# Second attention: keys in banks of 424, 424 and 254, and the context's sums over the whole third bank

## The chip, the core and the metric

The kernel runs on one NeuronCore of a Trainium2 chip, as one program. The metric is device microseconds (us) of one execution. The engines of the core are named as in the profile: PE is TensorE's matmul side, PEld its weight loads, DVE VectorE, ACT ScalarE, POOL GpSimd, SP SyncE. PSUM is the memory that PE writes, 128 partitions of eight banks; a bank holds 512 float32 columns, and one matmul writes inside one bank.

## What is computed

The program is a transformer of two layers over `x` (2 batches x 1024 tokens x 256): attention to a context of 77 tokens, a mixture of experts, a second attention, and a second mixture. The change touches the second attention alone. Cut to what matters, the reference is:

```python
xn = layernorm(ctx);  ln = layernorm(latents)            # 77 context tokens, 1024 latents
q  = (ln @ Wq)                                           # 16 heads of 64
kv = concatenate([xn @ Wkv, ln @ Wkv], axis=1)           # keys and values: 77 + 1024
qn = rmsnorm(q, qn_g) * scale;  kn = rmsnorm(k, kn_g)
sim  = einsum('bhid,bhjd->bhij', qn, kn)
sim  = where(padded_mask, sim, max_neg)                  # the mask covers the 77 context keys only
attn = softmax(sim, axis=-1)
out  = einsum('bhij,bhjd->bhid', attn, v) @ Wout + bout
```

In the kernel the order of the keys is the other way round: first the 1024 latents, then the 77 of the context, 1101 in all (`KEYS`), padded by one zero column to 1102 (`W2`).

## The kernel before

**Tiling.** `layer1_attention` works on a pair of heads at a time: 2 batches x 8 pairs of heads are 16 "pairs". A pair has 16 units (`UNITS`); a unit is 128 queries of one head against all 1101 keys. The pairs are written out for the first and the last of a batch and run in a hardware loop for those between (`all_pairs`), so 4 of the 16 pairs are written-out code and 12 are loop code. In each pair the body goes over `u` = 0, 2, ... 14. I call one such pass a step and name it by its `u`: "step 8" is the pass with u = 8. The scores that it makes are those of units u+2 and u+3, so eight steps of two units make a pair, and 128 steps the attention.

**A unit's way.** Scores lie in a `slot` of three banks, and there are two slots, one for even and one for odd units.
1. PE, `score` (L1689): three column ranges, 0 to 512, 512 to 1024 and 1024 to 1102, one for each bank. Each takes two matmuls in float32r with the same stationary operand (the high and the low part of the keys as moving operand), so a unit has four matmuls of 512 columns and two of 78. After each range `bank_filled` goes up by one.
2. DVE, `peak` (L1880, L1882): the largest score of a row. One reduction over bank 0 (512 columns) as soon as one range is there, one over the other 589 as soon as three are, and a third small one over the two results, negated, into `npeak`.
3. ACT, `exponentials` (L1823, L1824): exp(score - peak) of 1024 latents with their sum (`latent_sum`), then of the 77 context keys without one.
4. DVE, `row_sum` (L1912): masked sum over the 77, added to `latent_sum`.
5. PE, `turn` (L1696, L1698): nine transposes of the probabilities back into the same slot; DVE `copy_first` (L1903) copies tiles 0 to 3 and ACT `copy_rest` (L1835) tiles 4 to 8 into `probT`.
6. PE, `weigh` (L1714): the values weighed by `probT`, a group of four units late, half a group in each step.

**Order of a step on PE** (written out by hand): turn(u), an output projection (L1731), turn(u+1), score(u+2), score(u+3), a piece of the next pair's projections (`FRONT`), weigh, another piece (`BEHIND`). score(u+2) waits until both copies of unit u have left the slot, score(u+3) until both of unit u+1 have (`probT_act`, `probT_dve`).
**On ACT:** copy_rest(u), copy_rest(u+1), the exponentials of u+2, the FRONT piece, the exponentials of u+3, the BEHIND piece.
**On DVE:** row_sum(u), row_sum(u+1), copies (in steps 2, 6, 10 and 14 `copy_sums`, L1927, stands ahead of them, and ACT's copy_rest(u) waits for it by `r_out`), peak(u+2), peak(u+3), in some steps `invert`, and the FRONT piece.

**The pieces share one bank**, `side`: PE fills it, ACT or ACT and DVE empty it, and the next piece on PE waits for that. Four of the steps have a BEHIND piece whose bank is emptied only in the same step, behind the exponentials of unit u+2:

- step 6: FRONT `Kta`, BEHIND `V0`. `V0` (L1639) waits for DVE's L1890, which waits for ACT's L1818.
- step 8: FRONT `Ktb`, BEHIND `V1`, the same way.
- step 10: FRONT `Ktc` (77 keys), BEHIND `Qta` (L1675), the same way.
- step 12: FRONT `Qtb`, BEHIND `V2`. `V2` waits for ACT's L1803. Behind L1803 POOL makes L1601 and L1603.

Steps 0 and 2 have FRONT and BEHIND pieces too, but of the longer kind; steps 4 and 14 have a FRONT piece only. The last pair has no pieces.

```python
FRONT = {0: "Ka", 2: "c", 4: "Qb", 6: "Kta", 8: "Ktb", 10: "Ktc", 12: "Qtb", 14: "V3"}
BEHIND = {0: "Kb", 2: "Qa", 6: "V0", 8: "V1", 10: "Qta", 12: "V2"}
```

Of the kernel before, what the change touches and what calls it, by code (L numbers as in the profile page):

```python
# [17 lines left out]
ALU = mybir.AluOpType  # L18
# [37 lines left out]
KT_TILES = SEQ // P + 1  # L56
PAIRS = H1 // 2
# [120 lines left out]
class Context:  # L178


    def __init__(self, nc, ctx):
        sb = lambda n, s, d=F32: ctx.enter_context(nc.sbuf_tensor(f"a1_{n}", s, d))
        self.ctxT = sb("ctxT", [P, EC, BATCH * CTX])
        self.valid = sb("valid", [CTX, BATCH])
        self.gamma = sb("gamma", [P, 1])
        self.maskf = sb("maskf", [P, BATCH, CTX])
        self.maskn = sb("maskn", [P, BATCH, CTX])
        self.lng, self.lnb = sb("lng", [P, EC]), sb("lnb", [P, EC])


class ContextPrelude:
# [35 lines left out]
    def statistics(self, dve):  # L227
        s, v, C = Steps(dve, self.step), self.nc.vector, self.C
        dve.wait_ge(self.loaded, 144)
        s.mark(v.tensor_copy(C.maskf[:, :, :], self.mask[:, :, :]))  # L230
# [1218 lines left out]
def layer1_attention(nc, I, xres, ident, C, latT, W, w_loaded, gates, y_rows):  # L1449
# [7 lines left out]
    with phase(nc) as outer:  # L1457
# [6 lines left out]
        ctxT, valid, gamma, maskf = C.ctxT, C.valid, C.gamma, C.maskf  # L1464
# [18 lines left out]
        part_peak = sb("part_peak", [P, 2, 2])  # L1483
        latent_sum = sb("latent_sum", [P, 2])
        masked = sb("masked", [P, CTX])
# [9 lines left out]
        sums, py = slot[0][:, SEQ + P:SEQ + 3 * P], slot[1][:, SEQ + P:SEQ + P + E]  # L1495
# [10 lines left out]
        NSET = 3  # L1506
        FOLDS = D1.bit_length() - 1
# [125 lines left out]
        def _(pe):  # L1633
# [44 lines left out]
            def score(pair, u):  # L1678
# [8 lines left out]
                for lo, hi in ((0, BANK), (BANK, SEQ), (SEQ, W2)):  # L1687
                    for part in range(2):
                        ins = t_.matmul(out[:, lo:hi], q, KHL[:, pair.parity, h, part, lo:hi],  # L1689
                                        start=part == 0, stop=part == 1)  # L1690
                    ins.then_inc(bank_filled, 1)
# [93 lines left out]
        def _(act):  # L1785
# [34 lines left out]
            def exponentials(pair, u):  # L1820
                act.wait_ge(peaked, pair.g * UNITS + (u + 1))
                bias = npeak[:, u % 2:u % 2 + 1]
                a_.activation(prob[:, u % 2, 0:SEQ], slot[u % 2][:, 0:SEQ], ACT.Exp, bias=bias, accum_out=latent_sum[:, u % 2:u % 2 + 1])  # L1823
                a_.activation(prob[:, u % 2, SEQ:KEYS], slot[u % 2][:, SEQ:KEYS], ACT.Exp, bias=bias).then_inc(exped, 1)  # L1824
# [40 lines left out]
        def _(dve):  # L1865
# [8 lines left out]
            def peak(pair, u):  # L1874
# [3 lines left out]
                for i, (lo, hi, banks) in enumerate(((0, BANK, 1), (BANK, KEYS, 3))):  # L1878
                    dve.wait_ge(bank_filled, n + banks)
                    v.tensor_reduce(part[:, i:i + 1], slot[u % 2][:, lo:hi], AX.X, ALU.max).then_inc(part_peaked, 1)  # L1880
# [25 lines left out]
            def row_sum(pair, u):  # L1906
# [5 lines left out]
                v.tensor_tensor_reduce(masked[:, :], prob[:, u % 2, SEQ:KEYS], maskf[:, pair.b, :], 1.0,  # L1912
# [193 lines left out]
```

## Time and profile before

| | |
|---|---|
| median of 3 runs | 2143.6 us (2143.26 to 2143.99) |
| the profiled execution | 2148.2 us, of which 2146.4 us are its span |
| PE / PEld busy, of the span | 1923.6 us (90%) / 1652.1 us (77%) |
| DVE / ACT / POOL busy, of the span | 1272.3 us (59%) / 1022.2 us (48%) / 609.7 us (28%) |
| granted clock of TensorE, mean | 0.941 |

The second attention is the long middle part of the span, where its lines run from about 630 to 1750 us. Busy times of matmuls overlap, since they are pipelined: the start of one weight load to the start of the next tells what a matmul costs in a row of them, its own duration does not. A timeline row gives start and length of a run of like instructions, their count, and in brackets the idle time of the engine before them and what ended it. What waits for what inside a step can be read as distances from the start of the step's first score load; I call that moment S.

### The profile page before, as it was taken

The numbers are of one execution on the slowest core, as the hardware profiler recorded it, in microseconds if no ns is written. First come the engines' busy times: TensorE is split into PE (matmuls) and PEld (weight loads), VectorE is DVE, ScalarE is ACT, GpSimd is POOL, SyncE is SP. The second block draws the span as 40 slices with busy tenths as digits, with TensorE's granted clock in tenths as the row PEclk, the third lists the DMA queues.
The fourth block names the chain that finished last, engine by engine and source line by source line (L and its number), as shares of the span: only waits on it lengthen the run. The fifth ranks groups of instructions, "written<-read, shape, count | busy, mean of one in ns | idle before, by whom it ended". The sixth has DMA issues, their size and how long they took to land. (4 is left out here: it accounts for less than half of the span.)

```text
span 2146.4 us, 40118 instructions
## 1 busy us (share of the span) xinstructions
PE 1923.6 (90%) x13656; PEld 1652.1 (77%) x13657; DVE 1272.3 (59%) x2963; ACT 1022.2 (48%) x1747; POOL 609.7 (28%) x555
## 2 busy tenths in 40 slices
PE   4788957999569999999999999999999984899994
PEld 2477956999558887888888888878888863899994
DVE  5174054676656776777776677767777775122223
ACT  2543413555236555555555555555555641444441
POOL 2300002333244323432343224322433201222220
PEclk9899957999769999999999999999999995999997
DMA  5502163111242123211321132213211208211113
GB/s 201 176 28 82 64 239 104 47 49 46 84 106 53 38 51 71 54 42 47 70 54 43 45 70 63 47 33 70 64 45 33 63 23 298 90 37 34 39 35 130
DMA packets 93663, 159.24 MB, mean 74 GB/s; under 512 B 22385, under 2 KB 54831, under 8 KB 91707
## 3 DMA queue, kind: packets, MB, share of 16 engines
q1 hardware_dynamic: 82875, 134.32, 22.2%
q0 software_dynamic: 8320, 20.65, 3.2%
q8 instruction: 101, 1.65, 0.3%
q10 hardware_dynamic: 2304, 2.10, 0.3%
q14 instruction: 63, 0.52, 0.1%
HBM read 71.57 MB, written 32.41 MB: 48 GB/s over the span
## 5 line engine op out<-in xcount | busy, mean ns | idle before, releaser
L1880 DVE TENSOR_REDUCE a_part_peak<-a_slot 128x1 f32<-128x512 f32 (+1 forms) x512 | 352.6, 728 | 41.2 <-PE a_slot L1689 40.8
L1823 ACT ACTIVATE a_prob<-a_slot,a_npeak 128x1024 f32<-128x1024 f32 x256 | 286.0, 1117 | 176.5 <-DVE a_npeak L1882 176.2
L1689 PE MATMUL a_slot<-a_KHL,a_QHL 128*128 128x512 f32 (+1 forms) x1536 | 319.9, 358 | 2.3 <-ACT a_latT L1257 2.3
L1689 PEld LDWEIGHTS a_slot<-a_KHL,a_QHL 128*128 128x128 f32 x1536 | 261.9, 191 | 48.7 <-ACT a_latT L1257 2.6
L1714 PE MATMUL a_po<-a_probT,a_V 128*64 128x256 f32 (+1 forms) x2304 | 276.8, 385 | 0.0
L1835 ACT ACTIVATE a_probT<-a_slot 128x640 f32<-128x640 f32 x256 | 180.7, 706 | 200.2 <-PE a_slot L1698 182.1
L1698 PE MATMUL a_slot<-ident,a_prob 128*128 128x128 f32 x2048 | 266.1, 273 | 0.0
L1698 PEld LDWEIGHTS a_slot<-ident,a_prob 128*128 128x128 f32 x2048 | 233.7, 142 | 8.5 <-issue 0.2
L1639 PE MATMUL a_side<-a_W,a_latT 128*128 128x128 f32 x1536 | 214.1, 291 | 13.5 <-DVE a_KT L1890 5.8
L1639 PEld LDWEIGHTS a_side<-a_W,a_latT 128*128 128x128 f32 x1536 | 190.0, 199 | 45.9 <-DVE a_KT L1890 19.2
L1714 PEld LDWEIGHTS a_po<-a_probT,a_V 128*64 128x64 f32 (+1 forms) x2304 | 154.0, 136 | 82.2 <-issue 10.3
L1903 DVE COPY a_probT<-a_slot 128x512 f32<-128x512 f32 x256 | 176.7, 690 | 29.8 <-PE a_slot L1698 28.7
L1912 DVE CUSTOM_DVE_ANT_0 a_masked<-a_prob,a_maskf,a_latent_sum 128x77 f32<-128x77 f32 x256 | 124.6, 487 | 117.4 <-ACT a_prob L1824 100.2
L1068 PEld LDWEIGHTS m1e_ph<-m1e_xT,m1e_w 128*128 128x128 f32 x1248 | 148.7, 196 | 8.6 <-DMA m_down<-in_L_ffn_W_dram 3.6
L1068 PE MATMUL m1e_ph<-m1e_xT,m1e_w 128*128 128x128 f32 x1248 | 149.2, 279 | 6.1 <-DMA m_down<-in_L_ffn_W_dram 3.4
L1068 PEld LDWEIGHTS m0e_ph<-m0e_xT,m0e_w 128*128 128x128 f32 x1248 | 147.9, 195 | 6.0 <-ACT m0e_w L1095 3.3
L1068 PE MATMUL m0e_ph<-m0e_xT,m0e_w 128*128 128x128 f32 x1248 | 148.4, 278 | 3.4 <-ACT m0e_w L1095 2.9
L1077 PE MATMUL m1e_py<-m_down,m1e_h 128*128 x624 | 141.0, 379 | 0.0
L1580 POOL TENSOR_TENSOR a_square<-a_knat 128x1152 f32<-128x1152 f32 x15 | 31.6, 2108 | 368.0 <-ACT a_V L1808 368.0
L1133 DVE TENSOR_TENSOR m1e_h<-m1e_ph,m_bup 128x1024 f32<-128x1024 f32 x39 | 47.8, 1225 | 142.8 <-PE m1e_ph L1068 142.8
L1077 PEld LDWEIGHTS m1e_py<-m_down,m1e_h 128*128 128x128 f32 x624 | 115.6, 190 | 14.1
L1586 POOL TENSOR_TENSOR a_square<-a_square 128x576 f32<-128x576 f32 (+3 forms) x180 | 104.2, 579 | 14.1
(319 smaller groups left out, 2884.8 us busy)
## 6 DMA issues: line engine op xcount, KB each, us to landing
a_KHL<-a_KT SPq DMA_DIRECT2D x128, 256.0 KB, 4.5
a_QHL<-a_QT SPq DMA_DIRECT2D x128, 128.0 KB, 2.3
m_up<-_L_ffn_gate_up_proj_dram SPq DMA_DIRECT2D x8, 1024.0 KB, 8.7
m_up<-in_L_ffn_W_dram SPq DMA_DIRECT2D x8, 1024.0 KB, 9.1
m_down<-in_L_ffn_W_dram SPq DMA_DIRECT2D x8, 1024.0 KB, 12.5
a_prob_dram<-a0p_zeros SPq DMA_DIRECT2D x4, 1632.0 KB
a_dist_dram<-a_dist SPq DMA_DIRECT2D x4, 1632.0 KB, 8.1
a_band_prob<-a_prob_dram SPq DMA_DIRECT2D x4, 1632.0 KB, 6.8
```

Source lines behind the costliest of these rows:

```text
L1068: ins = nc.tensor.matmul(ph[:, q, cols], w[:, q, c, cols], xT[:, c, :], start=c == 0, stop=c == EC - 1)
L1077: ins = nc.tensor.matmul(py[1 - q][:, 0:E], a[:, 1 - q, f * P:(f + 1) * P], down[:, bass.ds(e, 1), f, :].rearrange("p a n -> p (a n)"), st ...
L1586: g_.tensor_tensor(half[:, :, 0:w], half[:, :, 0:w], half[:, :, w:2 * w], ALU.add).then_inc(summed, 1)
L1639: ins = t_.matmul(out, x[:, c, :], W[:, parity, i, c, :], start=c == 0, stop=c == EC - 1)
L1689: ins = t_.matmul(out[:, lo:hi], q, KHL[:, pair.parity, h, part, lo:hi], start=part == 0, stop=part == 1)
L1698: ins = t_.transpose(out[:, j * P:(j + 1) * P], prob[:, u % 2, j * P:(j + 1) * P], ident[:, :])
L1714: ins = t_.matmul(po_t[h * D1:(h + 1) * D1, :], V[0:rows, pair.parity, j, h, :], probT[0:rows, gi % 2, j, h, :], start=j == PARTS[0][0], s ...
L1823: a_.activation(prob[:, u % 2, 0:SEQ], slot[u % 2][:, 0:SEQ], ACT.Exp, bias=bias, accum_out=latent_sum[:, u % 2:u % 2 + 1])
L1835: a_.activation(probT[:, u // 4 % 2, HALF:KT_TILES, h, u % 2 * P:(u % 2 + 1) * P], slot[u % 2][:, HALF * P:KT_TILES * P].rearrange("p (t q ...
L1880: v.tensor_reduce(part[:, i:i + 1], slot[u % 2][:, lo:hi], AX.X, ALU.max).then_inc(part_peaked, 1)
L1903: v.tensor_copy(probT[:, u // 4 % 2, 0:HALF, h, u % 2 * P:(u % 2 + 1) * P], slot[u % 2][:, 0:HALF * P].rearrange("p (t q) -> p t q", q=P)) ...
L1912: v.tensor_tensor_reduce(masked[:, :], prob[:, u % 2, SEQ:KEYS], maskf[:, pair.b, :], 1.0, latent_sum[:, u % 2:u % 2 + 1], ALU.mult, ALU.a ...
```

## The change

The columns of a unit's scores are cut at 424 and 848 in place of 512 and 1024 (`CUT` = 424), so that the three banks hold 424, 424 and 254 columns; 253 of the last (`REST`) are keys, 176 latents and the 77 of the context. The place of a bank in the slot stays. With that:

- `score` has four matmuls of 424 columns and two of 254 a unit; their number stays.
- `peak` reduces banks 0 and 1 in one instruction (2 x 424 into two results) once **two** ranges are there, where it was 512 once one was there; then the 253 of the third bank once three are there; then the three results.
- The first exponential takes 848 columns from two banks, with their sum, the second 253.
- `row_sum` works on 253 probabilities in place of 77. Its mask, `maskr`, has ones for the 176 latents, set once by a memset long before.
- `sums` and `py`, which borrow the end of a slot's third bank, move to its last 256 columns, clear of the 254.

Nothing stands in another order on any engine. The diff, cut to its core:

```diff
+CUT = 424
+REST = KEYS - 2 * CUT
...
-        s.mark(v.tensor_copy(C.maskf[:, :, :], self.mask[:, :, :]))
+        s.mark(v.memset(C.maskr[:, :, 0:REST - CTX], 1.0))
+        s.mark(v.tensor_copy(C.maskf, self.mask[:, :, :]))
...
-        sums, py = slot[0][:, SEQ + P:SEQ + 3 * P], slot[1][:, SEQ + P:SEQ + P + E]
+        sums, py = slot[0][:, 3 * BANK - 2 * P:], slot[1][:, 3 * BANK - E:]
...
+        def two_banks(x):
+            return x[:, 0:2 * BANK].rearrange("p (n k) -> p n k", n=2)[:, :, 0:CUT]
...
-                for lo, hi in ((0, BANK), (BANK, SEQ), (SEQ, W2)):
+                for i, (lo, hi) in enumerate(((0, CUT), (CUT, 2 * CUT), (2 * CUT, W2))):
                     for part in range(2):
-                        ins = t_.matmul(out[:, lo:hi], q, KHL[:, pair.parity, h, part, lo:hi],
+                        ins = t_.matmul(out[:, i * BANK:i * BANK + hi - lo], q, KHL[:, pair.parity, h, part, lo:hi],
                                         start=part == 0, stop=part == 1)
                     ins.then_inc(bank_filled, 1)
...
-                a_.activation(prob[:, u % 2, 0:SEQ], slot[u % 2][:, 0:SEQ], ACT.Exp, bias=bias, accum_out=latent_sum[:, u % 2:u % 2 + 1])
-                a_.activation(prob[:, u % 2, SEQ:KEYS], slot[u % 2][:, SEQ:KEYS], ACT.Exp, bias=bias).then_inc(exped, 1)
+                a_.activation(prob[:, u % 2, 0:2 * CUT].rearrange("p (n k) -> p n k", n=2), two_banks(slot[u % 2]),
+                              ACT.Exp, bias=bias, accum_out=latent_sum[:, u % 2:u % 2 + 1])
+                a_.activation(prob[:, u % 2, 2 * CUT:], slot[u % 2][:, 2 * BANK:2 * BANK + REST], ACT.Exp, bias=bias).then_inc(exped, 1)
...
-                for i, (lo, hi, banks) in enumerate(((0, BANK, 1), (BANK, KEYS, 3))):
-                    dve.wait_ge(bank_filled, n + banks)
-                    v.tensor_reduce(part[:, i:i + 1], slot[u % 2][:, lo:hi], AX.X, ALU.max).then_inc(part_peaked, 1)
+                dve.wait_ge(bank_filled, n + 2)
+                v.tensor_reduce(part[:, 0:2], two_banks(slot[u % 2]), AX.X, ALU.max).then_inc(part_peaked, 1)
+                dve.wait_ge(bank_filled, n + 3)
+                v.tensor_reduce(part[:, 2:3], slot[u % 2][:, 2 * BANK:2 * BANK + REST], AX.X, ALU.max).then_inc(part_peaked, 1)
...
-                v.tensor_tensor_reduce(masked[:, :], prob[:, u % 2, SEQ:KEYS], maskf[:, pair.b, :], 1.0,
+                v.tensor_tensor_reduce(masked[:, :], prob[:, u % 2, 2 * CUT:], maskr[:, pair.b, :], 1.0,
                                        latent_sum[:, u % 2:u % 2 + 1], ALU.mult, ALU.add,
```

## Rows read from the trace of the kernel before

**Rows 1.** Windows, the attention's steady stretch: bounds and length, busy, granted clock, DMA

```profile
700.00:1746.00 1046.00, 1035.24 (x7781) 857.42 (x7780) 769.81 (x1858) 588.42 (x1164) 360.72 (x308) 1.00 0.22 51
```

**Rows 2.** Waits, same stretch: engine and line, for whom, us in all, times, longest

```profile
PEld a_side L1639 <- DVE a_KT L1890: 14.5, 28, 0.7
```

**Rows 3.** Groups by form, same stretch: count, busy us, mean ns, idle before

```profile
L1880 DVE TENSOR_REDUCE a_part_peak<-a_slot 128x1 f32<-128x512 f32 x239 | 165.1, 691 | 25.9 <-PE a_slot L1689 25.6
L1880 DVE TENSOR_REDUCE a_part_peak<-a_slot 128x1 f32<-128x589 f32 x239 | 183.1, 766 | 0.0
L1823 ACT ACTIVATE a_prob<-a_slot,a_npeak 128x1024 f32<-128x1024 f32 x238 | 265.9, 1117 | 162.9 <-DVE a_npeak L1882 162.7
L1824 ACT ACTIVATE a_prob<-a_slot,a_npeak 128x77 f32<-128x77 f32 x238 | 77.5, 326 | 0.0
```

**Rows 4.** Line L1689 (ns min/median/max), then its third, sixth and seventh load in step 8

```profile
L1689 PE MATMUL a_slot<-a_KHL,a_QHL x1536: 197/392/775, 633.2 to 1746.1; 128*128 128x512 f32 x128, 128*128 128x78 f32 x64
...
1102.80 0.19 PEld L1689 LDWEIGHTS a_slot<-a_KHL,a_QHL 128*128 128x128 f32 x1
...
1103.51 0.19 PEld L1689 LDWEIGHTS a_slot<-a_KHL,a_QHL 128*128 128x128 f32 x1
...
1103.62 0.19 PEld L1689 LDWEIGHTS a_slot<-a_KHL,a_QHL 128*128 128x128 f32 x1
```

**Rows 5.** Timeline, step 8 of a loop pair, from its first score load: start, us

```profile
1102.46 2.39 PEld L1689 LDWEIGHTS a_slot<-a_KHL,a_QHL 128*128 128x128 f32 x12
...
1102.77 0.71 ACT L1835 ACTIVATE a_probT<-a_slot 128x640 f32<-128x640 f32 x1 [0.71 <-PE a_slot L1698]
...
1103.23 1.40 DVE L1880 TENSOR_REDUCE a_part_peak<-a_slot 128x1 f32<-128x512 f32 x2 [0.20 <-PE a_slot L1689]
...
1104.85 1.12 ACT L1823 ACTIVATE a_prob<-a_slot,a_npeak 128x1024 f32<-128x1024 f32 x1 [1.38 <-DVE a_npeak L1882]
```

**Rows 6.** Timeline, step 8, its end: the keys' low part and V1

```profile
1106.79 0.69 DVE L1890 TENSOR_TENSOR a_KT<-a_side,a_KT 128x512 fp32r<-128x512 f32 x1 [0.32 <-ACT a_KT L1818]
...
1107.54 0.63 PEld L1639 LDWEIGHTS a_side<-a_W,a_latT 128*128 128x128 f32 x5 [0.66 <-DVE a_KT L1890]
```

**Rows 7.** Timeline, step 6: S, the keys' low part and V0

```profile
1093.94 2.39 PEld L1689 LDWEIGHTS a_slot<-a_KHL,a_QHL 128*128 128x128 f32 x12
...
1098.27 0.69 DVE L1890 TENSOR_TENSOR a_KT<-a_side,a_KT 128x512 fp32r<-128x512 f32 x1
...
1099.17 0.63 PEld L1639 LDWEIGHTS a_side<-a_W,a_latT 128*128 128x128 f32 x5 [0.38 <-DVE a_KT L1890]
```

**Rows 8.** Timeline, step 10: S, the context keys' low part and Qta

```profile
1111.04 2.39 PEld L1689 LDWEIGHTS a_slot<-a_KHL,a_QHL 128*128 128x128 f32 x12
...
1115.28 0.23 DVE L1890 TENSOR_TENSOR a_KT<-a_side,a_KT 128x77 fp32r<-128x77 f32 x1
...
1115.90 0.42 PEld L1675 LDWEIGHTS a_side<-ident,a_qnat 128*128 128x128 f32 x4 [0.39 <-issue]
```

**Rows 9.** Timeline, step 12 to the S of step 14

```profile
1118.69 2.39 PEld L1689 LDWEIGHTS a_slot<-a_KHL,a_QHL 128*128 128x128 f32 x12
...
1122.40 0.69 ACT L1803 ACTIVATE a_qgam<-a_side,a_gamma 128x512 f32<-128x512 f32 x1
...
1123.49 0.97 PEld L1639 LDWEIGHTS a_side<-a_W,a_latT 128*128 128x128 f32 x8 [0.39 <-ACT a_qgam L1803]
...
1124.28 1.27 POOL L1603 TENSOR_TENSOR a_QT<-a_qgam,a_QT 128x512 fp32r<-128x512 f32 x1
...
1124.43 1.22 DVE L1912 CUSTOM_DVE_ANT_0 a_masked<-a_prob,a_maskf,a_latent_sum 128x77 f32<-128x77 f32 x1 [1.58 <-ACT a_prob L1824]
...
1126.11 0.71 ACT L1835 ACTIVATE a_probT<-a_slot 128x640 f32<-128x640 f32 x1 [1.03 <-DVE a_rT L1927]
...
1127.03 2.36 PEld L1689 LDWEIGHTS a_slot<-a_KHL,a_QHL 128*128 128x128 f32 x12
```

**Rows 10.** Timeline, step 14 to the next turn

```profile
1132.72 0.14 PEld L1696 LDWEIGHTS a_slot<-ident,a_prob 128*77 128x77 f32 x1 [0.38 <-ACT a_prob L1824]
```

More of the change, by code:

```diff
@@ L185, in __init__ @@
         self.gamma = sb("gamma", [P, 1])
-        self.maskf = sb("maskf", [P, BATCH, CTX])
+        self.maskr = sb("maskr", [P, BATCH, REST])
+        self.maskf = self.maskr[:, :, REST - CTX:]
         self.maskn = sb("maskn", [P, BATCH, CTX])
@@ L1463, in layer1_attention @@
         sem = lambda n: nc.alloc_semaphore(f"a1_{n}")
-        ctxT, valid, gamma, maskf = C.ctxT, C.valid, C.gamma, C.maskf
+        ctxT, valid, gamma, maskr = C.ctxT, C.valid, C.gamma, C.maskr
         W2 = KEYS + 1
@@ L1482, in layer1_attention @@
         probT = sb("probT", [P, 2, KT_TILES, 2, 2 * P])
-        part_peak = sb("part_peak", [P, 2, 2])
+        part_peak = sb("part_peak", [P, 2, 3])
         latent_sum = sb("latent_sum", [P, 2])
-        masked = sb("masked", [P, CTX])
+        masked = sb("masked", [P, REST])
         rsum = sb("rsum", [P, 2, 2, 2])
```

## Prediction

> **What bounds the kernel now.** I read the windows first: in the attention's steady stretch PE is busy 1035 of 1046 us, at the full clock (1.00, the 2.4 GHz level), DVE 770 and ACT 588 [rows 1]. So a step is as long as PE's work in it, unless PE waits inside. The waits tell where it does: 28 times for DVE's L1890, 14.5 us in all [rows 2]. That is the bank `side`, in steps 6 and 8 of 14 pairs. The timeline then shows how near the others are. I measure from S, the start of a step's first score load, and take a loop pair, as 12 of the 16 are.
>
> **What PE saves.** In step 8 the third load starts at 1102.80, the sixth at 1103.51, so a 512-column matmul costs 0.71/3 = 0.235 us; the sixth to the seventh load, behind 78 columns, 0.11; the unit takes 1103.62 - 1102.46 = 1.16 [rows 4, 5]. The 0.11 is the pace of the loads, since 78 columns themselves need less: the durations are 392 ns (512) and 197 ns (78) at the same latency, so a column costs 195/434 = 0.449 ns, and 78 columns some 0.04 [rows 4]. A matmul of 424 then costs 0.235 - 88 x 0.449 ns = 0.195, one of 254 0.04 + 176 x 0.449 ns = 0.116. The change takes 4 x 0.040 = 0.16 from a unit and adds 2 x 0.005, leaving 1.01. Its idea is in this: columns are moved from matmuls that cost by the column to ones that cost the load's pace. Two units a step save 0.30, 128 steps 38 us, if nothing else binds.
>
> **What takes some of it at once: score(u+3).** It waits for ACT's copy of unit u+1, which starts 0.31 behind S and ends at 1102.77 + 0.71 = S + 1.02 [rows 5]. From an end to PE's next load I take 0.06, as from L1890's end, 1107.48, to V1's load, 1107.54 [rows 6]. So the second unit can't start before S + 1.08; now it starts at S + 1.16, afterwards it would like S + 1.01. Both units end at 1.08 + 1.01 = 2.09, where it was 2.33 or 2.34: a step saves 0.25, not 0.30. In the four written-out pairs the copy starts some 0.06 later, and the saving is 0.19.
>
> **What the Vector chain adds.** DVE's first reduction starts at S + 0.77, when bank 0 is filled [rows 5]. Afterwards it waits for four matmuls in place of two. Before, the second matmul streamed until third load + 0.235 = S + 0.34 + 0.235 = 0.575. Afterwards the fourth streams from 0.11 + 3 x 0.195 = 0.695 until 0.89. The start moves by 0.31, to S + 1.08. The work behind it stays: 691 + 766 ns for 589 + 512 columns [rows 3] become, at the slope of these two (75 ns for 77 columns), 1.02 + 0.44, the same 1.46. The exponentials too: 1117 + 326 ns give 0.835 ns a column, so 0.97 + 0.47, the same sum [rows 3]. So all that stands behind the first peak (the exponentials from S + 2.39 [rows 5], L1818, L1890, L1803) comes 0.31 later, counted from S, while PE comes 0.25 earlier. Where the two meet inside a step, the step ends by the late one:
>
> - **Step 6.** L1890 ends at 1098.96, V0 is loaded at 1099.17, S + 5.23: a slack of 0.21, 0.15 with the 0.06 [rows 7]. Afterwards V0 can be loaded at 5.02 + 0.31 + 0.06 = 5.39. The step gets 0.16 **longer**.
> - **Step 8.** PE waits already; all of the 0.31 is added: 0.31 **longer** [rows 6].
> - **Step 10.** L1890 ends at 1115.51 = S + 4.47, Qta at S + 4.86 [rows 8]. Afterwards 4.84: 0.02 shorter.
> - **Step 12.** L1803 ends at 1123.09 = S + 4.40, V2 at S + 4.80 [rows 9]. Afterwards V2 can go at 4.77: 0.03 shorter. But there is a longer chain: L1803, then POOL's L1601 and L1603, the latter until 1125.55; DVE's row_sum, two inputs in SBUF, takes 1.22 us and ends at 1125.65, 0.10 behind POOL [rows 9]. I read that as DVE waiting for POOL's end. Then L1927 and ACT's copy_rest(u), which ends at 1126.82, 0.21 ahead of the next S (1127.03) [rows 9]. Afterwards POOL ends 0.31 later, and row_sum has 176 more columns, at 0.97 ns 0.17 more: 0.48 in all against a slack of 0.21 - 0.06. The step gets 0.33 **longer**. With S this late, ACT's copy of the second unit no longer binds in step 14, which saves 0.31.
> - **Steps 0, 2, 4, 14.** The turn or piece at the end waits for nothing near: in step 14 the turn comes at 1132.72 = S + 5.69 [rows 10], its exponentials end near S + 3.8, 4.1 afterwards, and the second unit's about 1.6 later, when turn(u+1) is a further 1.3 off. They save 0.25 each, 14 saves 0.31.
>
> The last chain hangs on what row_sum waits for. If its 1.22 us were not POOL's doing, POOL's shift would not reach PE, step 12 would get 0.03 shorter like step 10, and the sum below would be 15 x 0.36 = 5.4 us lower.
>
> The page SBUF — State Buffer of the Trainium skill (SBUF: two separate sides) states that a DVE instruction with two SBUF inputs and a GpSimd one that reads SBUF share one port as an exclusive lock, held for the whole instruction, whoever comes first. By that rule the longer row_sum can also hold POOL up, which speaks against the change; the end 0.10 behind POOL's agrees with it.
>
> **The sum.** A loop pair: -3 x 0.25 - 0.31 + 0.16 + 0.31 - 0.02 + 0.33 = -0.28. Twelve: -3.4. The three written-out pairs with pieces: the saving of steps 0, 2, 4 is 0.19 and of 14 0.25, so -0.04 each, -0.1. The last pair has no pieces: 7 x -0.19 = -1.3, and -0.3 for the two first units. The memset is outside and short. Together -5 us: the 38 are there, and 33 of them go again. Against the profiled execution of 2148.2 us that is 2143.2; against the median, which I forecast, 2143.6 - 5.0 = **2138.6**.
>
> What no row shows is bounded. A reduction and an exponential that read two banks with a gap: nothing more than by the column, or, as the 589 columns that cross a bank already cost no more than the slope, at most a tenth of a us each. I take nothing; each tenth on the chain costs four steps of fifteen pairs, 60 x 0.1 = +6 us. The row_sum of 253: from 0 (hidden behind POOL) to twice the slope, so step 12 gets 0.16 to 0.50 longer: -2.5 to +2.5 us. POOL's chain could also not bind at all: -5. A 254-column matmul: 0.11 to 0.13, 0 to +2 us.
>
> **Rivals.**
> - *PE's gain arrives.* If ACT and DVE were not in the way (the reduction starts early enough, the bank `side` is emptied in time), each step saves 0.25 to 0.30: -32 to -38 us, 2106 to 2112. For it: PE's 99% [rows 1]. Against it: V1 starts 0.06 behind L1890 already now [rows 6].
> - *The Vector chain takes more than PE gives: slower.* The place is the first reduction and exponential in steps 6 to 12; the price is 60 times what each extra amount e adds to the 0.31. At e = 0.08 the gain is gone, from e = 0.15 it is slower by over 0.2%; e = 0.2 gives 2138.6 + 12 = 2151. For it: two-bank patterns, a third partial result, a longer DVE instruction against POOL. Against it: the columns are the same and so is the number of instructions.
> - *Narrow float32r matmuls cost more a column.* If 254 columns took 0.22, what a 512-column one takes, the unit would be back at 1.22, the four free steps longer by 0.12, and steps 6 to 12 as long as reckoned or more: some +1.4 a pair, near 2165. Against it: the 78-column duration, which leaves room for one pass only [rows 4].
> - *The change does nothing*: the widths are in the code as it says; no chance worth a number.
>
> **How the numbers follow.** The forecast has 0.70, with its own range 2129 to 2147 by the bounds above; 0.37 of it lies under 2139.3, 0.31 within 0.2%, 0.02 above. The gain arriving in full or half: 0.10. The slower chain: 0.17, of which 0.12 over 2147.9 and 0.05 under. The narrow matmuls: 0.03. A measurement of this kernel can tell about 0.2%, 4.3 us, from no change. Faster 0.47, same 0.36, slower 0.17. The range of 2123 to 2152 leaves out the full gain, the narrow matmuls and the ends of the rest.
>
> **What the profile after would show.** Score loads 0.195 apart and 0.115 behind 254 columns, or not (rival 3). The second unit's first load at S + 1.08, behind ACT's copy. The first reduction at S + 1.08 and about 1.02 long; more would be e. PE waiting for L1890 in steps 6 and 8 with 28 waits that total some 14.5 + 28 x 0.4 = 26 us or more, and for L1803 and r_out's copy in step 12. Steps 6, 8 and 12 longer than before and 0, 2, 4, 14 shorter. It is wrong if steps 6 and 8 get shorter, or if the first exponential starts elsewhere than S + 2.70.

## The result, and the profile after

| | before | after |
|---|---|---|
| median | 2144.7 us (2143.3 to 2147.1, 6 runs) | 2154.2 us (2151.1 to 2156.8, 6 runs) |
| the profiled execution | 2148.2 us, span 2146.4 | 2153.8 us, span 2152.0 |
| first to last unit of the attention | 1110.7 us | 1115.2 us |

The change makes the kernel slower: the ratio is 1.0037, interval 1.0025 to 1.0048. Forecast were 5 us less; it became 8 us more by the ratio, 9.4 by the two medians, and 2154.2 lies above the range. ("First to last unit" is from the first load of the first unit's scores to that of the last two units.)

The windows row of the stretch of [rows 1], in the trace of after (bounds and length; busy us of PE, PEld, DVE, ACT, POOL; granted clock; DMA share and GB/s):

```profile
700.00:1746.00 1046.00, 1013.90 (x7754) 864.40 (x7754) 803.63 (x1850) 583.59 (x1158) 367.20 (x309) 1.00 0.23 51
```

PE is busy 21 us less than before, at the same clock, in a stretch of the same length. So the gain of the narrower matmuls is there, and PE stands idle for it: 32 us in place of 11. Where, the waits say (engine and line, for whom; us in all, times, longest; same stretch):

```profile
PEld a_side L1649 <- DVE a_KT L1902: 28.4, 28, 1.2
ACT a_probT L1846 <- DVE a_rT L1939: 23.4, 15, 1.6
```

The first answers to [rows 2]: the same 28 waits for the keys' low part, 28.4 us for 14.5. The second is `copy_rest(u)` waiting for the copy of 1/sum, which stands behind the row sum on DVE: 1.6 us at most, and 1.0 before.

The groups by form that answer to [rows 3] (count | busy us, mean ns | idle before):

```profile
L1890 DVE TENSOR_REDUCE a_part_peak<-a_slot 128x2 f32<-128x848 f32 x238 | 247.8, 1041 | 61.7 <-PE a_slot L1699 61.7
L1892 DVE TENSOR_REDUCE a_part_peak<-a_slot 128x1 f32<-128x253 f32 x237 | 97.1, 410 | 0.0
L1833 ACT ACTIVATE a_prob<-a_slot,a_npeak 128x848 f32<-128x848 f32 x237 | 229.8, 969 | 201.5 <-DVE a_npeak L1894 201.3
L1835 ACT ACTIVATE a_prob<-a_slot,a_npeak 128x253 f32<-128x253 f32 x236 | 111.2, 471 | 0.0
L1924 DVE CUSTOM_DVE_ANT_0 a_masked<-a_prob,a_maskr,a_latent_sum 128x253 f32<-128x253 f32 x237 | 161.6, 682 | 84.2 <-ACT a_prob L1835 69.7 <-issue 14.1
L1934 DVE COPY a_rwide<-a_rsum 128x256 f32<-128x256 f32 x59 | 21.1, 358 | 2.0
```

The reductions (1.04 and 0.41 us) and the exponentials (0.97 and 0.47) have the durations forecast; a gap between two banks costs nothing. The last two rows are the ones to keep in mind: the mean of the row sum contains some that take three times the usual, and the copy into `rwide`, which the change doesn't touch, has a mean of 358 ns.

**Step by step.** In what follows a step's length is the distance from its S to the next S, the median of the twelve loop pairs, in us. Worked out from the score loads of each trace:

| step | 0 | 2 | 4 | 6 | 8 | 10 | 12 | 14 | pair |
|---|---|---|---|---|---|---|---|---|---|
| before | 10.59 | 9.84 | 8.75 | 8.51 | 8.58 | 7.64 | 8.35 | 8.08 | 70.32 |
| forecast change | -0.25 | -0.25 | -0.25 | +0.16 | +0.31 | -0.02 | +0.33 | -0.31 | -0.28 |
| after, change | -0.26 | -0.20 | -0.26 | **+0.34** | +0.29 | +0.04 | **+0.46** | -0.29 | +0.13 |

Six of the eight are within 0.06 of the forecast. Steps 6 and 12 make 0.31 of the 0.41 us that the pair is above it.

Step 6 in the trace of after (timeline, a loop pair; answers to [rows 7]):

```profile
1095.66 2.14 PEld L1699 LDWEIGHTS a_slot<-a_KHL,a_QHL 128*128 128x128 f32 x12
...
1099.16 3.95 POOL L1596 TENSOR_TENSOR a_square<-a_square 128x512 f32<-128x512 f32 x6
...
1099.99 0.59 DVE L1934 COPY a_rwide<-a_rsum 128x256 f32<-128x256 f32 x1
...
1100.50 0.68 DVE L1902 TENSOR_TENSOR a_KT<-a_side,a_KT 128x512 fp32r<-128x512 f32 x1
...
1101.23 0.97 PEld L1649 LDWEIGHTS a_side<-a_W,a_latT 128*128 128x128 f32 x8 [0.93 <-DVE a_KT L1902]
```

The copy into `rwide` takes 0.59 us, and the keys' low part stands behind it on DVE. And the same stretch before, where the copy takes 0.29:

```profile
1096.66 3.85 POOL L1586 TENSOR_TENSOR a_square<-a_square 128x512 f32<-128x512 f32 x6
...
1097.98 0.29 DVE L1922 COPY a_rwide<-a_rsum 128x256 f32<-128x256 f32 x1
```

Of POOL's six folds the first runs in both kernels for 1.27 us: before from 1096.66 to 1097.93, so that the copy fell 0.05 behind its end; after from 1099.16 to 1100.43, across the copy's start.

Step 12 of the same pair in the trace of after (timeline; answers to [rows 9]):

```profile
1121.08 2.14 PEld L1699 LDWEIGHTS a_slot<-a_KHL,a_QHL 128*128 128x128 f32 x12
...
1125.07 0.69 ACT L1813 ACTIVATE a_qgam<-a_side,a_gamma 128x512 f32<-128x512 f32 x1
...
1126.95 1.28 POOL L1613 TENSOR_TENSOR a_QT<-a_qgam,a_QT 128x512 fp32r<-128x512 f32 x1
...
1127.10 1.41 DVE L1924 CUSTOM_DVE_ANT_0 a_masked<-a_prob,a_maskr,a_latent_sum 128x253 f32<-128x253 f32 x1 [1.40 <-ACT a_prob L1835]
...
1128.43 0.41 DVE L1939 COPY a_rT<-a_slot 128x256 f32<-128x256 f32 x1
...
1128.96 0.70 ACT L1846 ACTIVATE a_probT<-a_slot 128x640 f32<-128x640 f32 x1 [1.58 <-DVE a_rT L1939]
...
1129.89 1.19 PEld L1699 LDWEIGHTS a_slot<-a_KHL,a_QHL 128*128 128x128 f32 x7 [0.55 <-issue]
```

The chain is the one that the prediction describes, L1813, POOL's QT, the row sum, the copy of 1/sum, copy_rest, and now PE is idle 0.55 us ahead of the scores.

### The profile page after: what moved, and what is told of

It is laid out like the page before. It is cut to its first block and busy times, and to the rows that moved or that the text cites. A ratio compares the mean times of both kernels' runs of the same rounds, so it can differ in the third digit from the quotient of the medians.

```text
span 2152.0 us, 40077 instructions
## 1 busy us (share of the span) xinstructions
PE 1905.9 (89%) x13656; PEld 1664.5 (77%) x13657; DVE 1312.9 (61%) x2964; ACT 1018.9 (47%) x1747; POOL 616.1 (29%) x555
## 5 line engine op out<-in xcount | busy, mean ns | idle before, releaser
L1833 ACT ACTIVATE a_prob<-a_slot,a_npeak 128x848 f32<-128x848 f32 x256 | 248.2, 969 | 217.7 <-DVE a_npeak L1894 217.4
L1890 DVE TENSOR_REDUCE a_part_peak<-a_slot 128x2 f32<-128x848 f32 x256 | 266.4, 1041 | 79.7 <-PE a_slot L1699 79.6
L1699 PE MATMUL a_slot<-a_KHL,a_QHL 128*128 128x424 f32 (+1 forms) x1536 | 298.9, 343 | 6.3 <-ACT a_probT L1846 3.7
L1699 PEld LDWEIGHTS a_slot<-a_KHL,a_QHL 128*128 128x128 f32 x1536 | 268.6, 190 | 17.5 <-issue 6.7
L1924 DVE CUSTOM_DVE_ANT_0 a_masked<-a_prob,a_maskr,a_latent_sum 128x253 f32<-128x253 f32 x256 | 171.8, 671 | 90.6 <-ACT a_prob L1835 76.1
L1835 ACT ACTIVATE a_prob<-a_slot,a_npeak 128x253 f32<-128x253 f32 x256 | 120.6, 471 | 0.0
```

The lines of the kernel that those rows point to most:

```text
L1699: ins = t_.matmul(out[:, i * BANK:i * BANK + hi - lo], q, KHL[:, pair.parity, h, part, lo:hi], start=part == 0, stop=part == 1)
L1833: a_.activation(prob[:, u % 2, 0:2 * CUT].rearrange("p (n k) -> p n k", n=2), two_banks(slot[u % 2]), ACT.Exp, bias=bias, accum_out=latent ...
L1835: a_.activation(prob[:, u % 2, 2 * CUT:], slot[u % 2][:, 2 * BANK:2 * BANK + REST], ACT.Exp, bias=bias).then_inc(exped, 1)
L1890: v.tensor_reduce(part[:, 0:2], two_banks(slot[u % 2]), AX.X, ALU.max).then_inc(part_peaked, 1)
L1924: v.tensor_tensor_reduce(masked[:, :], prob[:, u % 2, 2 * CUT:], maskr[:, pair.b, :], 1.0, latent_sum[:, u % 2:u % 2 + 1], ALU.mult, ALU.a ...
```

## The experiments

Theory (formed once the profile after was read): the whole chain behind the first peak comes 0.3 us later, as forecast, and two places where DVE and POOL wait for each other add what was not reckoned. Rival: something general, so that reductions, exponentials or row sums are slower in all steps. Each table row below gives the change against before, by step, as above.

| | 0 | 2 | 4 | 6 | 8 | 10 | 12 | 14 | pair | first to last unit | median, ratio |
|---|---|---|---|---|---|---|---|---|---|---|---|
| after | -.26 | -.20 | -.26 | +.34 | +.29 | +.04 | +.46 | -.29 | +.13 | 1115.2 | 2154.2, 1.0037 [1.0025, 1.0048] |
| after_again | -.25 | -.20 | -.24 | +.34 | +.29 | +.04 | +.46 | -.28 | +.16 | 1115.0 | 2151.2, 1.0035 [1.0021, 1.0048] |
| late_first | .00 | .00 | .00 | +.29 | +.44 | +.20 | +.44 | .00 | +1.37 | 1134.3 | 2172.3, 1.0124 [1.0105, 1.0144] |
| three_reductions | -.25 | -.20 | -.25 | +.07 | -.03 | -.20 | +.15 | -.29 | -1.00 | 1094.2 | 2134.0, 0.9939 [0.9921, 0.9958] |
| sum_77 | -.26 | -.20 | -.24 | +.15 | +.29 | +.04 | +.28 | -.28 | -.22 | 1105.8 | 2145.9, 0.9998 [0.9985, 1.0011] |
| invert_behind | -.26 | -.20 | -.24 | +.14 | +.29 | -.20 | +.46 | -.29 | -.31 | 1109.5 | 2145.6, 0.9995 [0.9981, 1.0010] |
| three_invert | -.26 | -.20 | -.26 | -.18 | -.03 | -.20 | +.14 | -.29 | -1.28 | 1093.4 | 2130.7, 0.9935 [0.9916, 0.9955] |
| pool_short | -.26 | -.20 | -.24 | +.33 | +.30 | +.04 | -.12 | -.25 | -.38 | 1109.3 | 2144.1, 0.9996 [0.9978, 1.0015] |
| row_late | -.25 | -.20 | -.24 | +.33 | +.29 | +.62 | -.12 | -.24 | +.20 | 1114.5 | 2152.3, 1.0030 [1.0017, 1.0044] |
| row_late_14 | -.26 | -.20 | -.26 | +.34 | +.29 | +.04 | -.12 | -.25 | -.40 | 1107.4 | 2145.5, 0.9998 [0.9985, 1.0012] |
| before_moves | .00 | .00 | .00 | .00 | .00 | .00 | -.04 | +.01 | -.03 | 1113.6 | 2147.4, 1.0008 [0.9994, 1.0021] |
| best_14 | -.25 | -.20 | -.24 | -.18 | -.03 | -.20 | -.24 | -.25 | -1.59 | 1089.9 | 2124.1, 0.9899 [0.9881, 0.9918] |

The time outside the attention varies from profile to profile between 1030 and 1040 us, whatever the kernel. Read the steps for what an edit does, the attention's length to some 3 us, and the median for what the whole is worth.

after_again is the changed kernel once more, run beside the experiments:

> The changed kernel once more, unedited, to have it timed beside the kernel before on the same chip as the runs below, and a second profile. From the first profile the attention (first to last score load) is 4.5 us longer than before; so 4 to 9 us more in all, and the same step lengths within 0.02 us. If the rest of the program is longer as well, it shows in the second profile's stretches outside the attention; if that was chance, the difference nears 4.5.

It comes out the same step by step.

### The first reduction alone: late_first

Before, with one number changed.

```diff
-                for i, (lo, hi, banks) in enumerate(((0, BANK, 1), (BANK, KEYS, 3))):
+                for i, (lo, hi, banks) in enumerate(((0, BANK, 2), (BANK, KEYS, 3))):
```

> The kernel before with one edit: DVE's first reduction of a unit (512 columns) waits for two score ranges in place of one. Widths, matmuls and sums stay. Theory A (the wait on the second bank moves the whole Vector and Scalar chain, and PE meets it at the bank `side` and at the copies): the reduction starts at S + 1.24 in place of S + 0.77, 0.47 later; step 6 gets 0.3 to 0.5 us longer, step 8 0.47, step 10 0.14, step 12 0.47, the others 0; some 1.4 to 1.6 a pair, 21 to 26 us in all, near 2168. Rival B (PE is the bound, DVE's start is covered): within 2 us of the kernel before.

Measured: the peak ends 0.45 later (S + 2.80, before S + 2.35), and 23.6 us are added between the first and the last unit; steps 0, 2, 4 and 14 don't move at all. Step 8 takes the 0.44 whole, step 6 0.44 less the slack of 0.15. That is the forecast's mechanism with its slacks, on before's own widths. Step 8's keys, whose low part answers to [rows 6] (timeline; S = 1042.74):

```profile
1042.74 2.38 PEld L1689 LDWEIGHTS a_slot<-a_KHL,a_QHL 128*128 128x128 f32 x12
...
1047.51 0.69 DVE L1890 TENSOR_TENSOR a_KT<-a_side,a_KT 128x512 fp32r<-128x512 f32 x1 [0.32 <-ACT a_KT L1818]
...
1048.26 0.97 PEld L1639 LDWEIGHTS a_side<-a_W,a_latT 128*128 128x128 f32 x8 [1.11 <-DVE a_KT L1890]
```

It ends at S + 5.46, where it was S + 5.02. One thing is already against the forecast: step 12 also takes the whole 0.44, with no slack.

### The first reduction given back: three_reductions

After, with one reduction for each bank, so that the first starts when one bank is filled.

```diff
-                dve.wait_ge(bank_filled, n + 2)
-                v.tensor_reduce(part[:, 0:2], two_banks(slot[u % 2]), ...)
-                dve.wait_ge(bank_filled, n + 3)
-                v.tensor_reduce(part[:, 2:3], slot[u % 2][:, 2 * BANK:2 * BANK + REST], ...)
+                for i, wide in enumerate((CUT, CUT, REST)):
+                    dve.wait_ge(bank_filled, n + i + 1)
+                    v.tensor_reduce(part[:, i:i + 1], slot[u % 2][:, i * BANK:i * BANK + wide], ...)
...
```

> The changed kernel with three reductions a unit (424 after the first range, 424 after the second, 253 after the third) in place of 848 after two and 253 after three. Theory A: the first one starts near S + 0.70, the first peak is done at S + 2.36 as before the change, the second at 3.98 (0.11 later than before, one more instruction each). Steps 0, 2, 4, 14 keep their 0.2 to 0.3 of gain, step 6 is at -0.04 to +0.13 against before, step 8 at 0, step 10 at -0.22, step 12 at +0.19 (the wider row_sum): -1.05 a pair, some -16 us against before, 2128 to 2131. Rival C (the loss is DVE's added busy time, the wide row_sum): 256 more instructions on DVE make it no better than the changed kernel, 2154 or more.

The first reduction and the exponential, from an S of 1021.91 (timeline):

```profile
1022.61 1.43 DVE L1891 TENSOR_REDUCE a_part_peak<-a_slot 128x1 f32<-128x424 f32 x3
...
1024.27 0.97 ACT L1833 ACTIVATE a_prob<-a_slot,a_npeak 128x848 f32<-128x848 f32 x1 [1.34 <-DVE a_npeak L1893]
...
1025.99 0.57 DVE L1933 COPY a_rwide<-a_rsum 128x256 f32<-128x256 f32 x1
```

Three reductions take 1.43 us, two took 1.45: an instruction more costs nothing here, and the peak ends at S + 2.32 in place of 2.64. The kernel is 0.6% **faster** than before, 21 us between the first and the last unit less than after. So the narrower cut was worth its gain, and the late first reduction had spent it. Of the 21 us some 18 lie in the steps and 3 in stalls where the hardware loop turns, of which more below. The steps came as expected, -1.00 a pair for -1.05 and 16.5 us less than before between the first and the last unit for 16; step 6 stays 0.07 longer than before, and its copy still takes 0.57. That the median is 3 us above what was expected lies outside the attention, or in the scatter of the times.

### The copy ahead of the keys: invert_behind

After, with the reciprocals and their copy into `rwide` behind the FRONT piece on DVE.

```diff
-                    if u % 4 == 2:
-                        invert(pair, u // 4)
                     if after and u in BOUND_AT:
                         bound(after, BOUND_AT.index(u))
                     if after and u in FRONT:
                         piece(after, FRONT[u])
+                    if u % 4 == 2:
+                        invert(pair, u // 4)
```

> The changed kernel with DVE's `invert` (reciprocal, and the copy into rwide, SBUF to SBUF) behind the FRONT piece in place of ahead of it. In the changed kernel's step 6 this copy takes 0.59 us in place of 0.29, beside POOL's sum L1596, and the keys' low part L1902 ends at S + 5.51 where the shift alone would give 5.33. Theory D (that collision is what made step 6 longer by 0.34 and not 0.16): L1902 starts when ACT has its half, ends near S + 5.33, step 6 is 0.17 shorter, step 10 0.25 to 0.29 shorter (PE's own pace); 6 to 7 us less than the changed kernel, 2147 to 2148. Rival: ACT's own chain is later than reckoned, and the step stays.

Step 6, from an S of 1018.12 (timeline):

```profile
1021.61 3.76 POOL L1596 TENSOR_TENSOR a_square<-a_square 128x512 f32<-128x512 f32 x6
...
1022.74 0.69 DVE L1902 TENSOR_TENSOR a_KT<-a_side,a_KT 128x512 fp32r<-128x512 f32 x1 [0.45 <-ACT a_KT L1828]
...
1023.48 0.97 PEld L1649 LDWEIGHTS a_side<-a_W,a_latT 128*128 128x128 f32 x8 [0.73 <-DVE a_KT L1902]
...
1023.55 0.29 DVE L1934 COPY a_rwide<-a_rsum 128x256 f32<-128x256 f32 x1
```

L1902 runs 0.69 us beside the end of the first fold (until 1022.88) and the second (1022.96 to 1023.69), not held: one of its inputs comes from PSUM. The copy, from SBUF to SBUF, takes 0.29: it starts only 0.14 ahead of the second fold's end and ends 0.15 behind it. V0 is loaded at S + 5.36, and the step is 0.14 longer than before, where the forecast had 5.39 and 0.16. So the forecast's chain was right for step 6, and the excess of after is the copy. With three_reductions as well (three_invert) step 6 falls by 0.25 again:

> The changed kernel with three reductions a unit and `invert` behind the FRONT piece. Theory: in step 6 the keys' low part ends near S + 5.0 (5.25 with three reductions alone), the step is at -0.15 to -0.2 against before (was +0.07); step 10 at -0.25 (was -0.20). 0.25 to 0.3 a pair, 4 to 5 us less than three reductions alone: 2129 to 2131. Rival: POOL's port holds another DVE instruction of step 6 in the copy's place, and the step stays at +0.07.

Measured 2130.7 us, step 6 -0.18, step 10 -0.20: the two edits hardly touch each other.

### The longer row sum: sum_77

After, but the 176 latents of the third bank are left out of the row sum (and so of the denominator); it is as short as before.

```diff
-                v.tensor_tensor_reduce(masked[:, :], prob[:, u % 2, 2 * CUT:], maskr[:, pair.b, :], ...
+                v.tensor_tensor_reduce(masked[:, REST - CTX:], prob[:, u % 2, SEQ:KEYS], maskr[:, pair.b, REST - CTX:], ...
```

> The changed kernel with row_sum over the 77 context keys alone, so the 176 latents of the third bank are left out of the row's sum. Theory A: only step 12 has row_sum on its path, behind POOL: 0.17 less there, 2.5 us in all, 2151 to 2152. Rival C (the 0.18 us more of DVE in each of 256 units is the loss, 47 us of busy time): most of the difference to the kernel before goes, 2145 or less.

It brings 9.4 us between the first and the last unit, against the 2.5 expected from step 12's 0.17 alone. Step 12 gives 0.18, as it should, 2.7 in 15 pairs. The rest was not expected: step 6 is 0.19 shorter in the loop's pairs (2.4 with the first), the last pair 0.5 us, and 3.7 lie in four stalls where the hardware loop turns, which say nothing of the row sum. For step 6 the timeline (S = 1023.34) shows why:

```profile
1019.24 3.27 POOL L1580 TENSOR_TENSOR a_kinv<-a_kvar,a_expo 128x18 f32<-128x18 f32 x1 [3.35 <-DVE a_kvar L1909]
...
1026.65 3.73 POOL L1596 TENSOR_TENSOR a_square<-a_square 128x512 f32<-128x512 f32 x6
...
1027.67 0.40 DVE L1934 COPY a_rwide<-a_rsum 128x256 f32<-128x256 f32 x1
```

POOL's power of 18 numbers takes 3.27 us; in the trace of after the same one takes 3.46:

```profile
1091.57 3.46 POOL L1580 TENSOR_TENSOR a_kinv<-a_kvar,a_expo 128x18 f32<-128x18 f32 x1 [3.23 <-DVE a_kvar L1909]
```

A row sum that starts 0.11 ahead of the power runs beside it, and its 0.18 us more are what POOL loses. POOL's chain then reaches the first fold at S + 3.31 and not at S + 3.50 (1099.16 - 1095.66), and the copy is held for 0.1 us, not 0.3. Before, the fold began at S + 2.72.

The Trainium skill's page SBUF — State Buffer (SBUF: two separate sides) has this as one rule: DVE with two SBUF inputs, or in one of its two-port modes, and GpSimd take turns on one port, each for a whole instruction, and the one that comes later is blocked. The same page says that a float32 copy from SBUF to SBUF is of the two-port kind. The runs here agree in both directions, with 0.59 for 0.29 (the copy held by a fold) and 3.46 for 3.27 (the power held by the row sum). One thing does not agree. These are the two row sums beside the power of the trace of after (timeline):

```profile
1091.46 0.48 DVE L1924 CUSTOM_DVE_ANT_0 a_masked<-a_prob,a_maskr,a_latent_sum 128x253 f32<-128x253 f32 x1
...
1093.26 0.48 DVE L1924 CUSTOM_DVE_ANT_0 a_masked<-a_prob,a_maskr,a_latent_sum 128x253 f32<-128x253 f32 x1 [1.31 <-ACT a_prob L1835]
```

The second one starts in the middle of the power, which lasts until 1095.03, and is not held; nor are the other 44 row sums of that trace that start inside a power. The 43 that meet one of POOL's adds, squares or subtractions (all that start 0.15 us or more ahead of its end) end 0.28 us behind that end, every one. So the rule agrees with these, and for the power once it runs the measurement stands against it.

### What the row sum of step 12 waits for: pool_short, row_late, row_late_14

pool_short is after with POOL's low part of the queries (L1613) on 16 of 512 columns, outside the first pair; the output is then that of coarser queries.

> The changed kernel with POOL's L1613 (the queries' low part) on 16 of its 512 columns in the pairs after the first, so the rest of the low part isn't computed. It tests what ends the row_sum of 1.41 us in step 12. Theory A (DVE's two-input row_sum waits for the end of POOL's L1613): row_sum takes 0.48, copy_rest(u) is not late, step 12 falls from 8.80 to near 8.27, 0.5 less in 14 or 15 pairs, 7 to 8 us less than the changed kernel. Rival: row_sum is long for a reason of its own (its inputs come late), and step 12 stays at 8.8.

Step 12's end (timeline; S = 1045.30):

```profile
1051.16 0.22 POOL L1617 TENSOR_TENSOR a_QT<-a_qgam,a_QT 128x16 fp32r<-128x16 f32 x1
...
1051.31 0.48 DVE L1928 CUSTOM_DVE_ANT_0 a_masked<-a_prob,a_maskr,a_latent_sum 128x253 f32<-128x253 f32 x1 [1.40 <-ACT a_prob L1839]
...
1052.41 0.70 ACT L1850 ACTIVATE a_probT<-a_slot 128x640 f32<-128x640 f32 x1 [0.82 <-PE a_slot L1712]
...
1053.52 0.50 PEld L1703 LDWEIGHTS a_slot<-a_KHL,a_QHL 128*128 128x128 f32 x3
```

The same row sum takes 0.48 us in place of 1.41, and step 12 is 0.58 shorter. So it had waited for POOL and was not working for 1.41 us (before 1.22): the question that the prediction left open is settled as it was read.

row_late leaves POOL alone and moves the row sum: in the bodies with u = 2, 6, 10 and 14 row_sum(u + 1) stands behind copy_first(u).

```diff
-                    row_sum(pair, u + 1)
+                    if u % 4 == 0:
+                        row_sum(pair, u + 1)
                     if u % 4 == 2 and one_before[0]:
                         ...
                     copy_first(pair, u)
+                    if u % 4 == 2:
+                        row_sum(pair, u + 1)
```

> The changed kernel with row_sum(u+1) behind copy_first(u) in the steps with u = 2, 6, 10, 14, so that copy_sums, which ACT's copy_rest(u) waits for, doesn't stand behind it. Nothing is left out. Theory A: step 12 falls to about 8.27 as with the short POOL instruction, the others stay within 0.05: 7 to 8 us less than the changed kernel. Rival: the delay passes to DVE's copy of unit u+1 and the second score waits: step 12 stays above 8.6.

A miss: step 12 falls to 8.23 us as it should, and step 10 rises from 7.68 to 8.27, so that next to nothing is left. The timeline at the end of step 8 and the start of step 10 shows what happened:

```profile
1115.98 0.69 DVE L1915 COPY a_probT<-a_slot 128x512 f32<-128x512 f32 x1
1116.02 1.91 POOL L1602 TENSOR_TENSOR a_qnat<-a_qnat,a_qinv 128x1024 f32<-128x1024 f32 x1
...
1116.59 1.62 DVE L1924 CUSTOM_DVE_ANT_0 a_masked<-a_prob,a_maskr,a_latent_sum 128x253 f32<-128x253 f32 x1
...
1118.66 0.70 ACT L1846 ACTIVATE a_probT<-a_slot 128x640 f32<-128x640 f32 x1 [1.54 <-DVE xres L1951]
```

Moved 0.6 us down, the row sum of that body runs into another POOL instruction, the scaling of the queries, and takes 1.62 us. DVE's add into `xres` and its copy stand behind it, and ACT's copy of the second unit waits for that add (1.54 us). It ends at 1119.36, and only then can the second unit's scores go, at S + 1.89 in place of 1.07; the peak comes at S + 3.08. row_late_14 therefore moves the line in the body with u = 14 alone:

> After, with one line moved, and only in the body with u = 14, whose end is step 12's: row_sum(u + 1) stands behind copy_first(u) there. Theory (the widened row sum waits behind GpSimd's write of QT, and in the run that moved it in every second body the same sum ran into GpSimd's scaling of the queries at the end of step 8, 1.62 us for 0.56): step 12 is 8.23 us again (before 8.35, after 8.80) and step 10 stays at 7.68 (it was 8.27 with the line moved at u = 10 too). Pair 69.9 us, 8 us less than after over the attention: about 2144. Rival (the row sum has to lie somewhere, and costs its 0.5 us on VectorE wherever it stands): step 12 falls and step 14 rises by as much, 2151 as after.

Step 12 is 8.23 and step 10 is 7.68. The step's end (timeline; S = 1047.59):

```profile
1053.46 1.28 POOL L1613 TENSOR_TENSOR a_QT<-a_qgam,a_QT 128x512 fp32r<-128x512 f32 x1
1053.84 0.42 DVE L1939 COPY a_rT<-a_slot 128x256 f32<-128x256 f32 x1 [1.63 <-PE a_slot L1706]
...
1054.71 0.70 ACT L1846 ACTIVATE a_probT<-a_slot 128x640 f32<-128x640 f32 x1 [0.82 <-PE a_slot L1708]
1054.88 0.48 DVE L1924 CUSTOM_DVE_ANT_0 a_masked<-a_prob,a_maskr,a_latent_sum 128x253 f32<-128x253 f32 x1
```

The copy of 1/sum (input in PSUM) runs beside POOL and is not held, and the row sum comes when POOL is done. Its rival, that the row sum costs its time wherever it stands, falls: step 14 is 7.83 against 7.79.

### The three moves together: best_14

After with three reductions, the reciprocals behind the piece, and the row sum of u = 15 moved.

> After, with all three moves: three reductions, one for each bank; the reciprocals behind the split of KT's low part; the row sum of unit 15 behind the first copy of the context's transposes. Theory (the terms add, since each is taken from the end of a step of its own): step 6 -0.18, 8 -0.03, 10 -0.20, 12 from +0.14 with three reductions to about -0.40, 14 -0.29 against before; pair -1.8 us, 0.55 below three reductions with the reciprocals moved, so 8 us below its 2130.7: about 2123. Rival (with the first reduction early, step 12 is bound by GpSimd's QT and the last piece, not by the row sum): step 12 stays at +0.14 and the time at 2130.

2124.1 us, 1.0% faster than before and 1.4% faster than the change as it was. Step 12 fell less than expected, -0.24 and not -0.40, so the pair has -1.6 and not -1.8 us: there PE waits for `qgam` again (idle 0.38 us, before 0.39), and -0.40 would have been more than the 0.25 that PE saves in a step. The timeline, from an S of 1045.73:

```profile
1049.39 0.69 ACT L1813 ACTIVATE a_qgam<-a_side,a_gamma 128x512 f32<-128x512 f32 x1
...
1050.32 0.97 PEld L1649 LDWEIGHTS a_side<-a_W,a_latT 128*128 128x128 f32 x8 [0.38 <-ACT a_qgam L1813]
```

How much of it is the cut's? before_moves is the kernel before with the two moves alone (the reciprocals, and the row sum of u = 15).

> Before (banks of 512, 512 and 78), with the two moves that need no other cut: the reciprocals behind the split of KT's low part, and row_sum(15) behind the first copy. Theory (the moves only take away collisions that the new cut brought about; before, the copy into rwide runs in the gap between two of GpSimd's folds in 0.29 us, and PE's own work sets the end of step 12): no step changes by more than 0.05 us, 2146 us, so that all of the 22 us that the best version gains belong to the cut. Rival (the moves are a gain of their own): step 10 or 12 of before gets shorter by 0.1 to 0.2, 2142 us or less.

No step moves by more than 0.04 us, and the time is that of before. So both moves only undo what the new cut brings about, and the 21 us between the first and the last unit are the cut's: somewhat over half of the 38 that PE could save.

## Why the prediction was wrong

- **What PE saves, and the wait for ACT's copy: right.** Score units 1.01 us apart where nothing waits, the second unit at S + 1.07 (forecast 1.08), steps 0 and 4 shorter by 0.26 (0.25).
- **The first reduction 0.31 later: right.** It starts at S + 1.08, the peak ends at S + 2.64, 0.29 behind before's, and the first exponential starts at S + 2.67 (forecast 2.70). The extra e of the second rival is nil: no instruction of the chain is slower than forecast. late_first and three_reductions show this shift from both sides, as the largest cost of the change: 24 us added to before, 21 taken from after.
- **Step 8, +0.29 for +0.31, and step 10, +0.04 for -0.02:** right within 0.06. In step 10 the copy ahead of the piece counts too: invert_behind gives 0.24 there.
- **Step 6: the step that failed first.** "V0 can be loaded at 5.02 + 0.31 + 0.06 = 5.39": measured 1101.23 - 1095.66 = 5.57. The forecast shifted one chain as a whole and left POOL's where it was. But POOL's stands on its own clock: it was 0.78 later counted from S (fold at S + 3.50, before 2.72): 0.29 from the late peak and 0.25 from the shorter step 4 (both reckoned), 0.19 from the longer row sum (shown by sum_77). So it fell on a copy from SBUF to SBUF that it had missed by 0.05 us before. 0.18 x 12 loop pairs = 2.2 us; the written-out pairs in the middle have +0.15, as forecast.
- **Step 12: the term was right, the slack was not.** "0.48 in all against a slack of 0.21 - 0.06": the chain came 0.45 later (copy_rest ends at 1129.66, S + 8.58; before S + 8.13). But from its end to the scores' first load it now takes 1129.89 - 1129.66 = 0.23 us, with PE idle, not the 0.06 that V1 needs behind L1902. So before's 0.21 was no slack at all in the loop's pairs, and 0.13 x 12 = 1.6 us. It is a matter of the loop's code. In the trace of after it is 0.22 us from ACT's end to this load (0.23 by the rounded rows) in each of the twelve passes through loop code, and 0.05 in the three through written-out code, as here (timeline):

```profile
1199.15 0.71 ACT L1846 ACTIVATE a_probT<-a_slot 128x640 f32<-128x640 f32 x1 [1.49 <-DVE a_rT L1939]
...
1199.90 1.20 PEld L1699 LDWEIGHTS a_slot<-a_KHL,a_QHL 128*128 128x128 f32 x7 [0.29 <-ACT a_probT L1846]
```

  A pair's first score has two waits more than the others, for the DMAs of its keys and queries; in the loop's passes these had landed 1.7 us earlier or more. What takes PE the 0.17 us stays open. That it is these two waits, whose values are worked out from the loop's counter, is a guess that no run tests. In the two written-out pairs in the middle, where the slack was real, step 12 got 0.27 and 0.24 longer.
- **The last pair: a sign wrong.** Forecast "7 x -0.19"; its steps are alternately 0.35 longer and 0.07 shorter. Without pieces PE waits for the exponentials already, which come 0.28 later, and in every other step the row sum stands on the path ahead of the copy of 1/sum. The chain of such a step (timeline of after; the one in the pair's last steps but one):

```profile
1741.21 0.48 DVE L1924 CUSTOM_DVE_ANT_0 a_masked<-a_prob,a_maskr,a_latent_sum 128x253 f32<-128x253 f32 x1 [0.97 <-ACT a_prob L1835]
...
1741.62 0.42 DVE L1939 COPY a_rT<-a_slot 128x256 f32<-128x256 f32 x1
...
1742.07 0.71 ACT L1846 ACTIVATE a_probT<-a_slot 128x640 f32<-128x640 f32 x1 [0.89 <-PE a_slot L1706]
...
1742.83 0.30 PEld L1699 LDWEIGHTS a_slot<-a_KHL,a_QHL 128*128 128x128 f32 x2 [0.15 <-ACT a_probT L1846]
```

  With the short row sum these steps are 7.03 in place of 7.20 us (sum_77), before 6.86. Six steps of it are 0.8 us more where 1.1 less was forecast, a miss of 1.9.
- **The sum.** From the first to the last unit -5 was forecast and +4.5 measured. Of the 9.5, the loop pairs' 0.41 x 12 make 4.9 and the last pair 1.9. Another 2.0 are stalls where the hardware loop turns (every second pair), which the median by step leaves out: the third, eleventh and thirteenth pair have a step 14 that changes by 0.4 to 1.5 us more than the others', at the same places in both traces of after, and two other steps by 0.2 to 0.6 less. In them the wait is put down to "issue", an engine that waits for nothing that the profile shows; what moved them stays open. before_moves, whose steps are before's to 0.04 us, is 2.9 us longer from the first to the last unit by such stalls alone, so these 2.0 say nothing of the change. The rest is in the first pair (+0.4 for 0), ahead of it (+0.2 for -0.3) and, the other way, in the two written-out pairs in the middle (-0.5 for -0.1).
- **The range** held each unknown of its list, and no list held POOL's clock, the wait-up of PE and the last pair. The chance of 0.17 for slower was tied to one mechanism (e), which did not occur.

## What to carry over

When a change moves one chain against another, list every place where the two share something, not only the ones that wait today: an instruction that now falls 0.05 us behind its rival is a future collision, and the timeline of before shows such near misses. A slack is the distance from a release to the load that waits for it, less what the engine takes to go on after such a release. Take that second term from the same place in the code, in a case where the engine really stood idle there: taken from another place it was 0.06 us for 0.22 here, and the slack was none. And where narrower banks let an engine run on sooner, keep the first consumer waiting for one bank: here an instruction more cost nothing, and waiting for two banks in place of one cost 21 us.

## What the runs showed of the hardware

- A reduction or an exponential over two pieces of 424 columns with a gap of 88 costs what its columns cost (1041 and 969 ns).
- A float32 copy from SBUF to SBUF of 256 columns takes 0.29 us alone and 0.59 across the end of a GpSimd fold, ending 0.15 behind it; a copy from PSUM (L1939) and a subtraction with one input there (L1902) run beside GpSimd at their usual 0.42 and 0.69.
- A row sum of 253 columns with two SBUF inputs takes 0.48 us alone; where it meets a GpSimd add, square or subtraction it ends 0.28 behind that one's end (43 of 43 in the trace of after), and started inside a GpSimd power it is not held (45 of 45).
- A GpSimd instruction that is not touched at all gets longer when a DVE row sum has started just ahead of it: the power of 18 columns 3.27 with the short ones, 3.46 with the long.
- From the end of what PE waits for to its next load it took 0.05 us (behind L1902, behind the second unit's copy) in some places and 0.22 to 0.23 in another (behind step 12's copy_rest in the hardware loop; 0.05 in the same place of the written-out code).
